# Cross attention of a decoder layer: the four value products of a group of heads in one stretch instead of at three positions

## What is computed

```python
def _L0_xattn_ref(Q, K, V, mask, Wq, bq, Wk, bk, Wv, bv, Wo, bo):
    B, S, D, H = (2, 256, 128, 16)
    HD = D // H
    q = (Q @ Wq + bq).reshape(b, -1, H, HD).transpose(0, 2, 1, 3)
    k = (K @ Wk + bk).reshape(b, -1, H, HD).transpose(0, 2, 1, 3)
    v = (V @ Wv + bv).reshape(b, -1, H, HD).transpose(0, 2, 1, 3)
    scores = jnp.einsum('bhqd,bhkd->bhqk', q, k) / scale
    scores = jnp.where(mask == 0, -jnp.inf, scores)
    attn = jax.nn.softmax(scores, axis=-1)
    ctx = jnp.einsum('bhqk,bhkd->bhqd', attn, v)
    concat = ctx.transpose(0, 2, 1, 3).reshape(b, -1, H * HD)
    return concat @ Wo + bo

x = x + _L0_attn_ref(_layernorm(x), ...)
x = x + _L0_xattn_ref(_layernorm(x), ctx_1024, ctx_1024, mask, ...)
x = x + _L0_ffn_ref(_layernorm(x), ...)
```

## Time and profile before

| | us |
|---|---|
| median of 3 runs (lowest, highest) | 220.93 (220.23, 222.34) |
| span of the profiled execution, first to last instruction | 219.2 |
| PE busy | 202.3 |
| DVE busy | 163.7 |
| ACT busy | 126.4 |
| POOL busy | 90.6 |

### The profile page before, as it was taken

How to read it: one execution, slowest core, us unless ns; L and a number is a source line. 1 busy time by engine, 2 the same in 40 slices (tenths; PEclk the granted TensorE clock), 3 DMA queues, 4 the chain that set the end, 5 groups by cost and what they waited for, 6 DMA issues and landing times.

```text
span 219.2 us, 4318 instructions
## 1 busy us (share of the span) xinstructions
PE 202.3 (92%) x1536; PEld 147.0 (67%) x1536; DVE 163.7 (75%) x424; ACT 126.4 (58%) x297; POOL 90.6 (41%) x136
## 2 busy tenths in 40 slices
PE   7599999799999799699796999999898999999993
PEld 7346466576767467456463665666565899999993
DVE  2628657878687799567999999998995685548843
ACT  2325436767575485536694989989696532372220
POOL 1989703764747466400899930000120002711332
PEclk9979999999999999979999999999999999999999
DMA  5960735999552003300601500000000000000000
GB/s 156 376 176 0 191 48 67 138 111 137 82 151 94 0 0 89 59 0 14 204 1 36 111 0 0 3 1 3 1 0 3 0 3 1 3 0 24 3 0 24
DMA packets 11740, 12.67 MB, mean 58 GB/s; under 512 B 848, under 2 KB 10064, under 8 KB 11648
## 3 DMA queue, kind: packets, MB, share of 16 engines
q1 hardware_dynamic: 11480, 12.20, 25.8%
q0 software_dynamic: 96, 0.20, 0.4%
q10 hardware_dynamic: 144, 0.01, 0.1%
HBM read 10.96 MB, written 1.44 MB: 57 GB/s over the span
## 4 chain that ended last, share of the span: by engine, by line
PE 74%; DVE 14%; issue 4%; ACT 3%; POOL 2%; DMA 2%; POOLq 0%; DVEq 0%
PE ps L830 12%; PE ps L792 8%; PE ps L721 7%; PE ps L736 7%; PE ps L851 7%; PE ps L629 7%; PE ps L708 6%; PE ps L770 6%; PE ps L752 5%; PE ps L641 4%; DVE q_t L1040 3%; DVE x_hat L915 2%; DMA x_in<-in_x 2%; PE ps L808 1%; DVE prob_t L1113 1%
## 5 line engine op out<-in xcount | busy, mean ns | idle before, releaser
L446 POOL TENSOR_TENSOR prob<-prob,rec 128x512 f32<-128x512 f32 x32 | 32.6, 1041 | 29.6 <-DVE rec L1095 29.6
L1040 DVE CUSTOM_DVE_ANT_0 q_t<-ps,mask_add 128x512 f32<-128x512 f32 x64 | 41.3, 682 | 2.1 <-PE ps L752 2.1
L531 ACT ACTIVATE prob<-ps,low 128x256 f32<-128x256 f32 x64 | 29.5, 475 | 18.4 <-DVE low L1030 18.4
L556 ACT ACTIVATE q_t<-q_t,low 128x512 f32<-128x512 f32 x44 | 29.4, 719 | 10.4 <-DVE low L1040 10.4
L386 POOL TENSOR_SCALAR var_eps<-mean_var 128x2 f32<-128x2 f32 (+1 forms) x5 | 1.1, 226 | 68.3 <-DVE mean_var L907 68.3
L792 PE MATMUL ps<-ident,q_t 128*128 128x128 f32 x176 | 23.4, 275 | 3.9 <-DVE place_o L1113 2.0
L792 PEld LDWEIGHTS ps<-ident,q_t 128*128 128x128 f32 x176 | 19.9, 141 | 9.2 <-issue 4.5
L1030 DVE TENSOR_REDUCE low<-ps 128x2 f32<-128x512 f32 x32 | 20.5, 683 | 6.3 <-PE ps L708 6.2
L1110 DVE COPY prob_t<-ps 128x512 f32<-128x512 f32 x32 | 20.6, 683 | 2.8 <-PE ps L736 2.8
L541 ACT ACTIVATE q_t<-ps 128x512 f32<-128x512 f32 x18 | 10.6, 598 | 21.0 <-PE ps L830 21.0
L752 PE MATMUL ps<-k_stack,q_stack 72*128 72x512 bf16 x64 | 19.3, 386 | 1.6 <-issue 1.6
(11 more groups left out here) (167 smaller groups left out, 422.3 us busy)
## 6 DMA issues: line engine op xcount, KB each, us to landing
k_stack<-k_dram SPq DMA_DIRECT2D x9, 256.0 KB
q_stack<-q_dram SPq DMA_DIRECT2D x6, 192.0 KB
wg<-in_L_ffn_w_gate SPq DMA_DIRECT2D x1, 1024.0 KB, 20.3
wu<-in_L_ffn_w_up SPq DMA_DIRECT2D x1, 1024.0 KB, 27.9
k_dram<-prob SPq DMA_DIRECT2D x1, 768.0 KB, 3.6
prob_t<-in_ctx SPq DMA_DIRECT2D x2, 256.0 KB, 4.0
w_in<-in_L_attn_Wq SPq DMA_DIRECT2D x1, 512.0 KB, 6.3
w_in<-in_L_attn_Wk SPq DMA_DIRECT2D x1, 512.0 KB, 7.1
```

The lines of the kernel that those rows point to most:

```text
L446: nc.gpsimd.tensor_tensor(pr, pr, rec1[:, s % 2, r, :].unsqueeze(2).to_broadcast([P, C, S]), ALU.mult).then_inc(s_norm1, 1)
L531: e = nc.scalar.activation(prob1[:, s % 3, r, c * S:(c + 1) * S], ps[:, 2 * (s % 2) + r, c * S:(c + 1) * S], ACT.Exp, bias=low1[:, s % 2, ...
L556: nc.scalar.activation(prob2[n % 3][:, c, :], score2[n % 2][:, c, :], ACT.Exp, bias=low2[:, n % 2, c:c + 1], scale=-1.0).then_inc(s_exp2, 1)
L1040: nc.vector.tensor_tensor_reduce(out=score2[n % 2][:, c, :], in0=ps[:, 2 * (n % 2) + c, :], in1=mask_add[:, c, :], scale=1.0, scalar=3e38, ...
```

## The change

For groups 0 to 5, all four value products are issued at the end of step 4k+8. Before, two stood in step 4k+7, one in 4k+8 and one in 4k+9. Groups 6 and 7 keep their own entries.

```diff
 VALUES2 = {}
 for k in range(B * NG):
-    later = {B * NG - 2: (1, 1, 2, 2), B * NG - 1: (0, 0, 0, 0)}.get(k, (1, 1, 2, 3))
+    later = {B * NG - 2: (1, 1, 2, 2), B * NG - 1: (0, 0, 0, 0)}.get(k, (2, 2, 2, 2))
     for kc in range(KC):
         VALUES2.setdefault(HG * (k + 1) + LAG_T + later[kc], []).append((k, kc))
```

## The result

| us | before | after |
|---|---|---|
| median, first comparison (lowest, highest) | 220.81 (220.23, 222.34) | 224.27 (223.66, 226.33) |
| ratio, 95% interval | | 1.0166 (1.0107 to 1.0225) |
| the same in a second comparison, of 6 new executions | 220.93 | 224.88, ratio 1.0209 (1.0137 to 1.0281) |
| span of the profiled execution | 219.2 | 221.8 |
| that execution's own time | not recorded | 223.66 |

The change makes the kernel slower, by 3.5 us in the first comparison and by 4.0 us in the second; 4.0 was forecast. The medians are of all executions, while the ratios leave out those more than 1.5% above the fastest of their kernel (in the second comparison 14 of 23 before and 1 of 6 after, where the medians alone stand at 1.018; beside a later experiment also one of the kernel before at 1084.19 us).

What follows compares the result with a forecast made beforehand. PE led with three engines nearly level, DVE having 0.1 us of slack in eight; DVE would decide the new period. Terms of groups 1 to 5 gave +4.03 us: 220.93 + 4.0 = 224.9 us, range 222.6 to 226.5.

Steps and rivals of the forecast that it cites:

- What bounds the kernel: Middle of cross attention: PE busy 8.00 of 8.00 us, DVE 7.89, ACT 7.49; DVE's work per period 7.74 us.
- What is taken away: PE's value products cost 1.86 us a group instead of 2.14: 0.28 less in groups 0 to 5, 1.7 in all.
- The hole: DVE idle before the copy of head 4k+7, waiting for PE's turns: 1.06 to 1.45 us a group, 1.15 taken.
- greatest lead: PE as far ahead as DVE's bank allows, turns 0.80 us after the previous head's copy began: DVE idle 1.06 us.
- PE's waits for DVE in between: Sign of being right: between the idle times, PE waits for DVE to empty the bank; 0.80 us from copy to turns.
- The sum: Period stretches between DVE copies, groups 1 to 5: +0.67, +0.98, +0.92, +0.68, +0.78; together +4.03 us.
- The projection in front of head 23: Group 4: the output projection of 0.45 us on PE stands behind the values and widens DVE's idle time of 1.15.
- Group 0 was taken as free: Its 1.29 us of added values end inside PE's 1.95 us gap while DVE splits queries: 0; uncovered, one more microsecond.
- nothing to win by the clock: Granted clock is 1.00 even where PE is busy only 16.12 of 19.60 us, so no clock gain is left.
- A: PE decides throughout and batching wins: 0.28 us off in six groups, 219.2 us; chance 0.05.
- B: DVE's idle times partly close, to 0.2 to 0.3 us a group: +0.1 in five groups, 221.4 us; chance 0.11.
- C: ACT's wait before o_raw adds to DVE's: half of 1.3 us in five groups, 3.2 more, 228.1 us; chance 0.04.

Runs made afterwards that it cites:

- apart: Kernel before, with groups 0 to 5 at later = (1, 1, 3, 3): two stretches of two value products with an ordinary step between; ratio 1.0073 to before.
- run with late outputs: Changed kernel, but outputs of groups 0 to 5 (o_raw, their turns, reciprocals, scaling) stay one step later, in step 4k+10; ratio 1.0190, median 223.67 us.
- groups 4 and 5 alone: Kernel before, with only groups 4 and 5 having their four value products in one stretch; one execution, 223.00 us.
- run of groups 1 to 3: Kernel before, with only groups 1 to 3 having their four value products in one stretch; median of four 224.06 us, traced execution 220.63 us.

## Why the prediction was right

**What bounds the kernel.** Right: three engines nearly level, with DVE 0.1 us short of full. Half of the value products left out brought the period from 7.91 to DVE's 7.65 only.

**What is taken away.** The 0.28 us of each group exist: the stretches last 1.86 us in the chain, for 2.14 before. They are worth nothing, since PE waits elsewhere; fewer stretches without a long one (apart) were slower too. By the Trainium skill (TensorEngine Tiling, Key Properties) a change of the tiling mode drains TensorE. The 0.14 us of each separate stretch agree with that, and they don't decide the time.

**The hole.** Right in place, cause and number of groups, a little short in size. By the reckoning from the copy of head 4k+5 the copy of head 4k+7 comes at 4.72; it came at 134.29 - 129.39 = 4.90. The turns of head 14 began 0.83 after that copy (0.80 reckoned), and the copy of head 15 began 0.64 after its turns, as reckoned. But from turns to turns it was 133.65 - 130.22 = 3.43 us and not 3.28. The term that was mis-sized is the one for the turns of head 14: from their own start they took 1.19 us and not 1.04 (1.17 and 0.88 in the chain), since ACT's copy of the head before, out of the other bank, was not finished. So two steps that should be 3.66 us lasted 4.90: 1.24 more, of which 1.18 is idle time in front of the copy. The prediction asked only what DVE's bank allows, and PE's second four turns hang on ACT's. Group 5 of the run with late outputs confirms it: there ACT's copy was over in time, the turns took 1.06 and DVE's idle time was 1.05, the 1.06 of the prediction's greatest lead. So the 1.15 came out near 1.18 in part by luck: it was chosen between 1.06 and 1.45 for a lead that is not whole, and the lead was whole; what was added is ACT's bank. The same 1.17 us of turns stands in the chain of the run with half of the work, whose hole was 0.32 instead of 0.2. PE's waits for DVE in between were there too, 0.83 us from copy to turns in every group, though in groups 1 to 4 the profile names ACT for this wait.

**The sum.** Groups 1 to 4: 3.56 us measured, 3.25 reckoned. The projection in front of head 23 widened the hole as reckoned (1.62 us of idle time, 1.15 + 0.45). Group 5: 0.78 reckoned, 0.67 without the clock's fall (from the run with late outputs). Together 4.2 at full clock, 4.0 reckoned, and the medians say 3.5 and 4.0 us. Group 0 was taken as free and costs 0.2 us by itself. Nothing was won back behind head 29, as said.

**What was missing** is the clock in group 5. It adds 0.9 to 1.4 us there, the difference between 10.22 to 10.65 and the 9.29 us at full clock. It was found in all four traces that have groups 4 and 5 in one full stretch with early outputs, and in none of the other ten. Then the measured difference should be above 5; it is not. Falls in other places (near 92 and 117 us) come and go from trace to trace and cost about as much (1.4 us in the trace of before, 1.1 in that of groups 4 and 5 alone). The one near 117 us stands in none of the three traces of the changed kernel and in two of the four with the old group 0 and full work, so the change may also save one. That such falls hide the difference is likely but not shown, and part of the agreement of 4.0 with the medians is luck. Whether the fall belongs to the change is likely too but not settled: the run with late outputs and the one with half of the work in the changed order had PE as idle in front of the place, and the clock held. The prediction had found nothing to win by the clock, from a window in which it was at 1.00; it did not ask what the new idle time of PE might lose by it.

**Rivals.** A fell with the first trace, and for its reason with the run of groups 1 to 3. B fell: the idle time before heads 11, 15 and 19 is 1.18 us in every trace of the changed kernel. C fell by the run with late outputs, though ACT's wait before o_raw (0.82 us) is there.

## What to carry to other kernels

An engine order is worth judging by the longest piece of work between two hand-overs to the engine that is nearly full, not by the number of pieces: here 0.28 us of switching saved cost 1.18 us of idle time on another engine. How much may come in a row follows from how far ahead the engine can be: with one bank of lead, DVE's work in hand was two steps of 1.83 us less the hand-over, and what came beyond it came out as idle time, one for one (0.85 us of stretch, 0.86 us of hole). Every engine that empties a buffer counts in this sum: ACT's bank added 0.13 us that DVE's alone would not have. A long stretch is cheap where the other engines have nothing to wait for, as at the end of the stage, or beside a long piece of their own work (group 0, which cost 0.2 us).

## What the runs showed of the hardware beside that

In the three traces of the changed kernel the periods at full clock repeat to 0.01 us, while its executions differ by 2 us and more. What differs between the traces is above all at which places TensorE's granted clock falls to half for some 2 to 4 us. In the two falls read more closely the place followed some microseconds in which PE was idle for much of the time (2.35 of 4 us busy ahead of 92 us in the kernel before; 2.37 of 4 ahead of the fall in the changed kernel), yet the same share of idle time did not always bring a fall (2.23 of 4 us busy in the run with late outputs, 2.35 of 4 from 154 us on in the changed order with half of the work, clock 1.00 in both). A hole that an order makes may thus cost a second time, in the clock of the work behind it; that it did so here is not shown.
